# Re-ordering the end of a merged recurrent/channel loop: moved VectorE steps, one shared table visit for the last two group norms

## The reference, cut to what matters

```python
out = scan over time of (r, k, v, w)                 # recurrence, 32 heads of 8
m = og.mean(-1); va = ((og - m) ** 2).mean(-1)       # group norm, per head
og = ((og - m) / sqrt(va + 1e-05)) * gn_w + gn_b
x1 = x + og * g @ Wo.T                               # gate, output projection, residual
xc = _ln(x1, ln2_w, ln2_b)                           # channel mix from here
sx2 = shift(xc) - xc
xk2 = xc + sx2 * ffn_maa_k;  xr2 = xc + sx2 * ffn_maa_r
rr = sigmoid(xr2 @ Wfr.T);   kk = square(relu(xk2 @ Wfk.T))
return x1 + rr * (kk @ Wfv.T)
```

## Time and profile before

| what | value |
|---|---|
| median of 3 runs (lowest, highest) | 1212.56 us (1209.41, 1212.6) |
| the profiled execution: its own time, its span | 1213.37 us, 1211.6 us |
| granted TensorE clock over the span | 0.982 of full speed |
| busy, share of the span: PE, DVE, ACT, POOL | 94%, 80%, 64%, 49% |
| chain that ended last: PE, DVE, issue | 69%, 14%, 13% |

### The profile page before, as it was taken

One profiled execution on the slowest core, in us unless ns is written; L12 is line 12 of the kernel. 1 busy time (PEld: TensorE's weight loads), 2 busy tenths in 40 slices (PEclk: granted clock), 3 DMA queues, 4 the chain that ended last, 5 costly groups with the idle time before them and its releaser, 6 DMA issues.

```text
span 1211.6 us, 35521 instructions
## 1 busy us (share of the span) xinstructions
PE 1136.8 (94%) x13568; PEld 963.8 (80%) x13568; DVE 969.1 (80%) x1677; ACT 777.1 (64%) x1752; POOL 593.9 (49%) x520
## 2 busy tenths in 40 slices
PE   5899999999999998999999999999999998987788
PEld 5889888888998877887788878888788876765667
DVE  5987778787777742288999999999999999999654
ACT  4778777777787754655665556655566546654464
POOL 4787787877877830333434333343434434233111
PEclk9999999999999989999999999999999999998899
DMA  9400000111111100000000000000000000000001
GB/s 334 130 4 1 0 1 3 29 38 47 40 39 43 35 2 1 1 1 1 2 1 1 1 1 1 0 0 0 0 0 0 0 2 1 18 9 9 18 28 60
DMA packets 25535, 27.31 MB, mean 23 GB/s; under 512 B 2336, under 2 KB 20064, under 8 KB 25056
## 3 DMA queue, kind: packets, MB, share of 16 engines
q1 hardware_dynamic: 25440, 25.99, 6.5%
HBM read 21.79 MB, written 4.19 MB: 21 GB/s over the span
## 4 chain that ended last, share of the span: by engine, by line
PE 69%; DVE 14%; issue 13%; POOL 2%; ACT 1%; DMA 0%; DVEq 0%; ACTq 0%; POOLq 0%
PE psum L945 9%; PE psum L353 9%; PE psum L954 7%; PE psum L267 5%; PE psum L1034 4%; PE psum L336 4%; PE psum L368 4%; PE psum L1071 3%; PE psum L297 3%; PE psum L280 3%; DVE shared L1723 3%; PE psum L1115 2%; PE psum L310 2%; DVE shared L1717 2%; PE psum L994 2%
## 5 line engine op out<-in xcount | busy, mean ns | idle before, releaser
L1723 DVE TENSOR_TENSOR_SCAN shared<-late_wT,shared 128x512 f32<-128x512 f32 x128 | 184.5, 1442 | 4.4
L856 POOL TENSOR_TENSOR late_xm<-late_mixed,late_xa 128x512 f32<-128x512 f32 x80 | 96.0, 1208 | 162.3 <-DVE late_mixed L1691 156.0
L232 POOL TENSOR_TENSOR shared<-shared,att_row_max 128x512 f32<-128x512 f32 x128 | 132.5, 1055 | 17.8 <-DVE att_row_max L564 17.8
L353 PE MATMUL psum<-shared 128*128 128x128 f32 x1024 | 127.3, 279 | 1.0 <-ACT shared L462 1.0
L453 ACT ACTIVATE shared<-shared 128x512 f32<-128x512 f32 x128 | 80.4, 631 | 69.7 <-POOL shared L232 69.6
L954 PE MATMUL psum<-w,late_hT 128*128 128x256 f32 x512 | 122.1, 383 | 1.0 <-ACT late_hT L1335 0.9
L353 PEld LDWEIGHTS psum<-shared 128*128 128x128 f32 x1024 | 121.4, 195 | 1.4 <-ACT shared L462 1.4
L865 POOL TENSOR_TENSOR shared<-shared,late_rT 128x512 f32<-128x512 f32 x32 | 40.7, 1273 | 164.0 <-DVE shared L1723 164.0
L945 PE MATMUL psum<-late_glnT,w 128*128 128x256 f32 x512 | 118.4, 385 | 1.8 <-ACT late_glnT L1326 1.8
L1717 DVE TENSOR_TENSOR shared<-psum,shared 128x504 f32<-128x504 f32 x128 | 86.7, 677 | 40.9 <-PE psum L1071 39.5
L564 DVE TENSOR_REDUCE att_row_max<-shared 128x8 f32<-128x512 f32 x128 | 86.7, 679 | 40.5 <-POOL shared L225 40.5
(11 more groups left out here) (160 smaller groups left out, 2672.0 us busy)
## 6 DMA issues: line engine op xcount, KB each, us to landing
shared<-in_enc SPq DMA_DIRECT2D x64, 128.0 KB, 2.6
out<-x SPq DMA_DIRECT2D x16, 256.0 KB, 2.0
x<-in_x SPq DMA_DIRECT2D x7, 512.0 KB, 9.5
w<-in_w SPq DMA_DIRECT2D x2, 1024.0 KB, 17.6
shared<-in_cross_mask SPq DMA_DIRECT2D x1, 1024.0 KB, 12.4
shared<-in_w_qkv SPq DMA_DIRECT2D x1, 768.0 KB, 4.7
x<-in_x SPq DMA_DIRECT2D x2, 256.0 KB, 3.9
shared<-in_w_kv SPq DMA_DIRECT2D x1, 512.0 KB, 13.2
```

Of the source, the lines that this page charges most:

```text
L232: nc.gpsimd.tensor_tensor(zs, zs, peak.unsqueeze(2).to_broadcast([P, PAIRS, S]), ALU.subtract).then_inc(shifted, 1)
L353: last = nc.tensor.matmul(dst[:, half * P:(half + 1) * P], w[:, kb, c0 + half * P:c0 + (half + 1) * P], src[:, u % 2, kb, 0:P], start=(kb ...
L856: nc.gpsimd.tensor_tensor(xm[:, m % 2, :, :].rearrange("p h (b t) -> p (h b) t", t=S), mixed[:, m % 2, :, :].rearrange("p h (b t) -> p (h ...
L1723: nc.vector.tensor_tensor_scan(states, wT[:, u, half, :, :, :].rearrange("p j b t -> p (j b t)"), states, 0.0, ALU.mult, ALU.add).then_inc ...
```

## The change

Four things are changed, all at the end of the loop.

- VectorE: in bodies 13 to 15 `add_residual(s-2)` moves from step 2 to step 1, ahead of `gate`. In body 15, `make_stats(13)`, `ch_variances(1)`, `centre(14)` and `sum_squares(14)` leave the body and stand behind it.
- ScalarE: in body 15 the two table loads, `invert_deviations`, `ch_invert(1)`, `square(14)` and `copy_on(14)` leave the body. Behind it, `square(14)` and `square(15)` come first, and then one visit of the Ln/Exp tables inverts run 14, run 15 and layer-norm part 1.
- Run 15's group norm has its own space in the weights of `w2`, which are no longer read: so `centred`, `squares`, `on`, the variance, its log and its inverse exist twice, and the norms of 14 and 15 can be under way together.
- Behind the last body the order of PE, ACT, DVE and POOL is written anew.

```diff
+        tail_space = core.weights["w2"]
+        centred_last, squares_last, on_last = (tail_space[:, i * RT * CH:(i + 1) * RT * CH] for i in range(3))
+        var_last, log_last, rstd_last = (tail_space[:, 3 * RT * CH + i * CH * RH:3 * RT * CH + (i + 1) * CH * RH]
+                                         for i in range(3))
...
@@ gpsimd
-                if there(s - 1):
+                if there(s - 1) and not s_is(s, RUNS - 1):
                     scale(s - 1)
...
             ch_shift(EARLY + 1, 1)
-            channel(EARLY, 0)
+            ch_shift(EARLY + 2, 0)
+            scale(RUNS - 2)
             scale(RUNS - 1)
-            channel(EARLY + 1, 1)
-            channel(EARLY + 2, 0)
+            ch_shift(EARLY + 3, 1)
+            ch_shift(EARLY + 4, 0)
...
@@ tensor
-                    if n == 7 and s_is(s, RUNS - 1):
-                        transpose_on(RUNS - 2)
...
             ch_values(EARLY - 1, 1)
-            project_out(RUNS - 2)
             ch_transpose(EARLY + 1, 1)
             ch_keys(EARLY, 0)
             sum_heads(RUNS - 1, 2)
             sum_heads(RUNS - 1, 3)
+            ch_receptances(EARLY, 0)
             transpose_o(RUNS - 1)
-            ch_receptances(EARLY, 0)
             channel(EARLY, 0)
-            channel(EARLY + 1, 1)
+            ch_transpose(EARLY + 3, 1)
+            ch_keys(EARLY + 2, 0)
+            transpose_on(RUNS - 2)
+            ch_values(EARLY + 1, 1)
+            ch_receptances(EARLY + 2, 0)
+            project_out(RUNS - 2)
+            ch_transpose(EARLY + 4, 0)
+            ch_keys(EARLY + 3, 1)
             transpose_on(RUNS - 1)
-            channel(EARLY + 2, 0)
+            ch_values(EARLY + 2, 0)
+            ch_receptances(EARLY + 3, 1)
             project_out(RUNS - 1)
...
@@ scalar
+            def invert_heads(r):
+                act.wait_ge(var_ready, r + 1)
+                if is_last(r):
+                    src, log, dst = var_last, log_last, rstd_last
+                else:
+                    src, log, dst = moments[:, 2 * CH:], log_var[:, CH:], rstd[:, CH:]
+                    act.wait_ge(on_ready, r)
+                nc.scalar.activation(log, src, ACT.Ln, bias=core.eps[:, :]).then_inc(logged, 1)
+                act.wait_ge(logged, r + 4)
+                nc.scalar.activation(dst, log, ACT.Exp, scale=-0.5).then_inc(rstd_ready, 1)
...
             bodies(act, body)
+            square(RUNS - 2)
+            ch_normalise(EARLY + 2, 0)
+            ch_copy_in(EARLY + 1, 1)
             ch_square(EARLY, 0)
             copy_o(RUNS - 1)
-            ch_copy_in(EARLY + 1, 1)
-            ch_normalise(EARLY + 2, 0)
             ch_tanh(EARLY, 0)
-            channel(EARLY, 0)
+            ch_copy_in(EARLY + 2, 0)
+            ch_normalise(EARLY + 3, 1)
+            ch_square(EARLY + 1, 1)
             square(RUNS - 1)
             nc.scalar.preload_act_table_set("natural_log_exp_and_others")
-            invert_deviations(RUNS)
+            invert_heads(RUNS - 2)
+            invert_heads(RUNS - 1)
+            ch_invert(1)
             nc.scalar.preload_act_table_set("gelu_apprx_tanh_and_others")
-            channel(EARLY + 1, 1)
+            ch_tanh(EARLY + 1, 1)
+            ch_copy_in(EARLY + 3, 1)
+            ch_normalise(EARLY + 4, 0)
+            ch_square(EARLY + 2, 0)
+            copy_on(RUNS - 2)
+            ch_tanh(EARLY + 2, 0)
...
@@ vector
+                    if n == 1 and early(s):
+                        add_residual(s - 2)
...
-            apply_gate(RUNS - 2, 0)
+            centre(RUNS - 2, 0)
             ch_finish(EARLY - 1, 1)
-            ch_shifts(1)
-            add_residual(RUNS - 2)
-            make_stats(RUNS - 2)
+            make_stats(RUNS - 3)
+            sum_squares(RUNS - 2)
+            ch_variances(1)
             ch_mix(EARLY + 1, 1)
             centre(RUNS - 1, 1)
             ch_mix(EARLY + 2, 0)
             sum_squares(RUNS - 1)
-            channel(EARLY + 1, 1)
-            apply_gate(RUNS - 1, 1)
-            channel(EARLY + 2, 0)
+            ch_finish(EARLY, 0)
+            ch_shifts(1)
+            apply_gate(RUNS - 2, 0)
+            ch_mix(EARLY + 3, 1)
+            ch_finish(EARLY + 1, 1)
+            add_residual(RUNS - 2)
+            make_stats(RUNS - 2)
+            ch_mix(EARLY + 4, 0)
+            apply_gate(RUNS - 1, 1)
+            ch_finish(EARLY + 2, 0)
             add_residual(RUNS - 1)
             make_stats(RUNS - 1)
```

More of the change, by code:

```diff
@@ L812, in early_run, with channel_runs @@
             return CH * (s - (RUNS - 3)) + i
-        def channel_runs(eng, body):
-            for s in range(EARLY + 4, RUNS):
+        def channel_runs(eng, body, start=EARLY + 4):
+            for s in range(start, RUNS):
                 body(s, s % 2)
@@ L1429, in square @@
                 act.wait_ge(centred_ready, r + 1)
-                if later(r):
-                    act.wait_ge(var_ready, r)
-                nc.scalar.activation(squares[:, :], centred[:, :], ACT.Square, scale=RS ** -0.5).then_inc(sq_ready, 1)
+                if is_last(r):
+                    src, dst = centred_last, squares_last
+                else:
+                    src, dst = centred, squares
+                    if later(r):
+                        act.wait_ge(var_ready, r)
+                nc.scalar.activation(dst[:, :], src[:, :], ACT.Square, scale=RS ** -0.5).then_inc(sq_ready, 1)
             def copy_on(r):
@@ L1601, in s_inverts @@
             def s_inverts(s):
-                return there(s + 2) or there(s - 1)
+                return there(s + 2) or there(s - 1) and not s_is(s, RUNS - 1)
             end = TILES - 1
@@ L1639, in _ @@
             nc.scalar.preload_act_table_set("gelu_apprx_tanh_and_others")
-            channel_runs(act, channel)
+            ch_normalise(EARLY + 7, 1)
+            ch_nonlinear(EARLY + 5, 1)
+            channel_runs(act, channel, EARLY + 5)
         @block.vector
@@ L1756, in centre @@
                 dve.wait_ge(mean_ready, r + 1)
-                if later(r):
+                if later(r) and not is_last(r):
                     dve.wait_ge(on_ready, r)
@@ L1868, in body @@
                     if n == 2:
-                        if there(s - 2):
+                        if there(s - 2) and not early(s):
                             add_residual(s - 2)
@@ L1877, in body @@
                         mix(s + 1, 1)
-                    if n == 3 and there(s - 2):
+                    if n == 3 and there(s - 2) and not s_is(s, RUNS - 1):
                         make_stats(s - 2)
@@ L1881, in body @@
                         ch_variances(0)
-                    if s_is(s, RUNS - 1) and n == 4:
-                        ch_variances(1)
                     if n == 4:
-                        if there(s - 1):
+                        if there(s - 1) and not s_is(s, RUNS - 1):
                             centre(s - 1, 1 - u)
@@ L1928, in _ @@
             ch_variances(2)
-            channel(EARLY + 3, 1)
+            ch_mix(EARLY + 5, 1)
+            ch_finish(EARLY + 3, 1)
             ch_shifts(2)
-            channel_runs(dve, channel)
+            ch_mix(EARLY + 6, 0)
+            channel_runs(dve, channel, EARLY + 5)
             ch_finish(RUNS - 1, 1)
```

39 lines of the change are left out of this document (26 added, 13 removed).

## The result

The changed kernel takes 1196.69 us, median of 6 runs (1194.93 to 1198.89); the kernel before, on the same chip, 1212.40 (1209.41 to 1212.79). The ratio is 0.9877, with a 95% interval of 0.9861 to 0.9892, or 15 us less. The forecast of 1202.3 had the direction right and the size too small: its range ended 1.1 us above the result. The profiled execution took 1195.06 us, with a span of 1193.3 and a mean granted clock of 0.990.

A forecast was written before the change was run, and what follows sets the result against it. TensorE's waits (16.6 us), released by DVE and ACT, and low clock behind them were taken as the bound. Waits -7.5, slow blocks -4.5, new slow blocks +1.8 gave -10.2 us: 1202.3 us, range 1197.8 to 1208.0.

The forecast's parts named there:

- The 4.19 us: TensorE's wait ahead of ch_receptances(5) for the relu, queued on ACT behind the inversion; to become 0.4 us.
- The start times behind `ch_keys(4)`: Counted from ch_keys(4): ch_keys(5) at about 11.0 us, transpose_o(15) at 25.0, project_out(14) at 39.8.
- the new waits: On TensorE: 2.0 us at transpose_o(15), 2.4 at project_out(14), 0.8 at ch_values(5), 0.25 for ch_mix(7).
- no drain: Table switches cost only their load; rival: two ahead of copy_on(14) cost 1.28 us more each, 1204.9 us, chance 0.03.
- what was moved on VectorE did not return: Rival: 4.7 us of moved DVE steps and 4.0 us of waits return behind body 15; 1211.0 us, chance 0.11.
- `add_residual` one step earlier: Fills part of DVE's 1.47 us wait at 1061.43; bounds nothing or 0.7 us, taken as 0.
- the upper bound of 0.7: Most that moving add_residual could gain, its own length on DVE, if no later transfer sets the body's pace.
- the prediction's own signs of being wrong: Late ch_mix(7) or shared visit, low clock where it was full, or over 1 us change before body 15.
- 4.5 us of slow blocks: Blocks behind removed waits, at 1128 to 1135 and 1170 to 1176, return to 1.89 us each: -4.5 us.
- 1.8 for new ones: Slow blocks charged once for the two new TensorE waits of about 2 us: +1.8 us.
- Two counts of one end: Besides the sum of -10.2 us, blocks and transposes counted behind project_out(14) put the last block 14.6 us earlier.
- the steps moved ahead of `ch_finish(4)`: make_stats(13), 0.73 us, and variances with centring, 2.96 us, leave DVE's queue, so DVE reaches ch_finish(4) 3.6 us earlier.

The follow-up runs named there:

- run 14: Not a follow-up: the kernel's own run RUNS - 2, whose norm is inverted in the shared table visit behind body 15; no separate time.
- experiment 5: Changed kernel with make_stats(13), ch_variances(1), centre(14), sum_squares(14) and square(14) back in body 15, inversion still behind it: 1199.92 us, ratio 0.9894 to the kernel before.
- experiment 1: Kernel before with only add_residual moved from step 2 to step 1 in bodies 13 to 15: 1209.21 us against 1213.03, ratio 0.9973.
- Experiment 3: Kernel before plus 20 unread identity transposes on TensorE ahead of its add_residual wait in bodies 13 and 14, nothing moved: 1208.35 us against 1212.37, ratio 0.9975.
- experiment 2: Changed kernel with add_residual back in step 2, all else of the change kept: 1201.04 us, ratio 0.9905 to the kernel before.
- experiment 6: Changed kernel with the shared table visit split in two, the first ahead of ch_square(7), with two more table loads: 1201.65 us, ratio 0.9917 to the kernel before.
- experiment 4: Kernel before plus 36 unread transposes on TensorE ahead of ch_receptances(5) in body 15, in its 4.19 us wait: 1210.91 us, ratio 0.9985.

## Why the prediction was right in direction and wrong in size

**Right: where the wait comes from.** The 4.19 us were ScalarE's queue behind the inversion: gone in the changed kernel and in experiment 5, where VectorE's steps are back and only the inversion is out of the body. The start times behind `ch_keys(4)` were right to 0.6 us, as shown above. That of `ch_keys(5)` is in part luck: `ch_keys(4)` took 1.99 us, not the 3.78 that were reckoned with, and a wait of 1.13 us that was not foreseen took its place.

**Right: the new waits.** 1.4 us at `transpose_o(15)` (2.0 predicted), 1.9 at `project_out(14)` (2.4), 0.8 and 0.2 at `ch_values(5)` and `ch_receptances(5)` (0.8 and 0.4). Two were larger than worked out: 1.1 us at `ch_keys(5)`, for which I had nothing, and 0.8 at `ch_keys(7)` (0.25). Two more were not in the sum, 0.7 us for POOL at the head sums (L1094) and 0.3 for `ch_normalise` (L1502). The wait at `ch_keys(5)` was masked in my working by a slow `ch_keys(4)`: I let `ch_finish(4)` wait for `ch_values(4)`, 8.4 us behind `ch_keys(4)`; with that block at full clock it is 6.6 us, and VectorE is late instead. The waits came to 7.7 us against 6.3.

**Right: no drain**, and what was moved on VectorE did not return: the waits for `ch_finish` behind `ch_keys(5)` that were 4.0 us are not in the list after.

**Wrong, and the cause of the miss: "`add_residual` one step earlier. [...] I take 0".** It is worth 3.3 us (experiment 1), and even the upper bound of 0.7 was far too low. I priced the idle time of VectorE that the step would fill. I did not ask who waits for `add_residual`: TensorE does, 2.76 us in each body. VectorE sets the pace in these bodies, so I took a wait of TensorE to be free. It is not: with the wait there, TensorE's clock is low at the start of the next body (0.65 and 0.69), and there VectorE does wait for it. Experiment 3 fills most of the wait, moves nothing, and gets 3.0 us. Two of the prediction's own signs of being wrong came true with it: the start of body 15 moved by 3.1 us (1092.98 to 1089.92, 1.1 of them from ahead of body 13), and the clock fell in a stretch that had it full (1064 to 1072).

**Mis-sized: the clock in the end.** I took back 4.5 us of slow blocks and charged 1.8 for new ones, in all -2.7. Taking the waits out of the column "to the last block", 83.5 us of the kernel before become 75.7, so -7.8 in that profile. 1.8 are the charge that did not fall due (no slow block follows the waits of 1.43 and 1.94 us), and 1.8 are `ch_keys(4)`, which I left slow (3.78, now 1.99), though part of that only becomes the wait at `ch_keys(5)`. The rest, about 1.5, is for the most part transposes and head sums in the slow stretches, which I did not count. Against this stand the 1.4 us more of waits. This term varies from profile to profile: in experiment 2 `ch_keys(7)` takes 3.57 us behind the same two waits, and in experiments 3, 5 and 6 other blocks are slow. So the timed 11.5 us of experiment 2 are the better measure of the end, 1.3 above the 10.2 predicted, with an interval that holds both.

**Two counts of one end.** The prediction also counted blocks, and had the end 14.6 us shorter; it called that the bound and gave the neighbourhood of it a chance of 0.05. In the profile the end is 13.9 us shorter (97.3 to 83.4), near that count, because no block there was slow. Two small slips change nothing: the steps moved ahead of `ch_finish(4)` are 0.73 + 2.96 = 3.7 us, not 3.6, and a bound of 14.6 us under the median before is 1198.0, not 1197.8.

Together: 10.2 predicted, 3.3 from `add_residual`, and 1.3 that are left for the end, which the profile lays to the clock and the times don't show apart from noise: 14.8 of the measured 14.9.

**Open.** Why the clock is low 29 us behind the wait of 2.76 us, no row shows, and the place is not fixed. The ten profiles have 20 starts of bodies 14 and 15. Where the wait is open (before, experiments 2 and 4), the block at the start is slow in 5 of 6; where it is gone or filled, in 1 of 14, the one of experiment 6. In experiment 4's profile body 14 starts at full clock and the slow stretch stands right behind its wait:

```profile
1047.63 1.89 PE L1034 MATMUL psum<-late_xm,WgT 128*128 128x256 f32 x8
...
1060.66 2.08 PE L994 MATMUL psum<-late_mixer_a,maa_w2a 32*128 32x256 f32 x8 [2.76 <-DVE x L1789]
```

VectorE then waits 1.9 us for TensorE there, and body 14 is as long as before (43.8). The wait for `scale` right ahead of body 15's start doesn't explain it alone: 2.37 us before with a slow block behind, 2.38 in experiment 3 and 2.03 in the changed kernel with a fast one. So the experiments show that the wait costs time, not the mechanism. Nor do I know why `ch_keys(4)` behind a wait of about 3 us is slow in some kernels (3.78 before, 3.16 in experiment 6) and not in others (1.99 after).

## What to carry to other kernels

A wait of 2 to 3 us on TensorE is not free because another engine sets the pace: look along the granted clock for slow stretches behind it, also some tens of us behind, at a place where that engine waits for TensorE. Price a moved step by who waits for it as well as by what it fills; and where such a wait can't be removed, a filler of short transposes that nobody reads is a cheap test, and here a gain. When an inversion with its table loads sits in a queue ahead of work that is urgent, first take it out of that queue. Merging two visits saved something more here, how much is not settled (0.8 us of wait, 5.0 by the medians, clock included).

## What the runs showed of the hardware

- 20 transposes of the identity (2.35 us of TensorE) in each of two waits that were there anyway made the whole kernel 3.0 us faster (interval 1.5 to 4.5).
- The length of a wait does not tell what follows it: 1.94 us at `project_out(14)` in the changed kernel is followed by 1.99 us, 2.77 at the same place in experiment 6 by 3.78, and the longest, 3.12 at `ch_keys(4)`, by 1.99 again.
- Body 13 started anywhere from 1004.7 to 1011.3 us in ten profiles, a spread larger than most single effects here, though no edit touches what stands ahead of it.
- A table load costs 1.29 us from its start to the next instruction's, to the Ln and Exp tables and back.
